# Segment sums in whole rounds of four blocks, message bases read behind the products, and one more picked tile in every third group of edges

## The reference, cut to what matters

```python
def _nnconv(x, src, dst, edge_attr, ew, eb, rw, rb):
    W = (edge_attr @ ew + eb).reshape(edge_attr.shape[0], x.shape[1], rw.shape[1])
    xj = x[src]
    msg = jnp.einsum('ei,eio->eo', xj, W)
    agg = jax.ops.segment_sum(msg, dst, num_segments=x.shape[0])
    return agg + x @ rw + rb
...
for i in range(N_LAYERS - 1):
    h = _nnconv(h, src, dst, edge_attr, edge_w[i], edge_b[i], root_w[i], root_b[i])
    h = _batchnorm(h, bn_gamma[i], bn_beta[i])
    h = jax.nn.relu(h)
h = _nnconv(h, src, dst, edge_attr, edge_w[-1], edge_b[-1], root_w[-1], root_b[-1])
```

## Time and profile before

| what | value |
|---|---|
| median of 3 runs | 7327.02 us (7326.24 to 7327.81) |
| profiled execution: its own time | 7327.42 us |
| its span, first to last instruction | 7325.4 us |
| mean granted TensorE clock, of 1 | 0.979 |
| PE busy | 7064.4 us (96%) |
| DVE busy | 6245.8 us (85%) |
| POOL busy | 5323.9 us (73%) |
| ACT busy | 4977.1 us (68%) |

### The profile page before, as it was taken

One profiled execution on the slowest core, in us unless ns is written; L12 is line 12 of the kernel. 1 busy time (PEld: TensorE's weight loads), 2 busy tenths in 40 slices (PEclk: granted clock), 3 DMA queues, 4 the chain that ended last, 5 costly groups with the idle time before them and its releaser, 6 DMA issues.

```text
span 7325.4 us, 131059 instructions
## 1 busy us (share of the span) xinstructions
PE 7064.4 (96%) x49442; PEld 6060.6 (83%) x49442; DVE 6245.8 (85%) x7568; ACT 4977.1 (68%) x8367; POOL 5323.9 (73%) x5635
## 2 busy tenths in 40 slices
PE   4999999999999899999999999989999999999998
PEld 3888888888888688888888888868888888888887
DVE  5888888888888788888888888878888888888885
ACT  4776667677767577676767677657767766676775
POOL 4777777777777477777777777757777777777774
PEclk7999999999999799999999999989999999999998
DMA  6111111111111111111111111111111111111111
GB/s 46 32 31 30 32 32 32 32 32 30 31 32 32 28 32 32 32 32 29 32 32 32 32 32 31 30 30 31 32 32 31 30 32 32 32 32 32 32 29 23
DMA packets 714221, 229.54 MB, mean 31 GB/s; under 512 B 573057, under 2 KB 664593, under 8 KB 713593
## 3 DMA queue, kind: packets, MB, share of 16 engines
q1 hardware_dynamic: 493253, 172.63, 10.6%
q0 software_dynamic: 180000, 46.44, 6.4%
q10 hardware_dynamic: 40340, 2.08, 0.7%
HBM read 217.19 MB, written 3.52 MB: 30 GB/s over the span
## 4 chain that ended last, share of the span: by engine, by line
PE 65%; POOL 17%; issue 8%; DVE 7%; DVEq 2%; ACT 0%; DMA 0%; POOLq 0%; ACTq 0%
PE bank L1128 52%; POOL xg L500 17%; PE bank L1095 8%; DVE xbig L688 2%; DVEq L778 2%; DVE spread L741 1%; DVE agg L783 1%; PE bank L1142 1%; PE bank L1141 1%; DVE agg L642 1%; PE bank L1199 1%; PE bank L1152 1%; PE bank L1154 1%; PE bank L1211 1%; DVE xg L746 0%
## 5 line engine op out<-in xcount | busy, mean ns | idle before, releaser
L500 POOL DMA_INDIRECT xg<-node_table,idx x5625 | 5323.1, 946 | 1927.5 <-issue 1777.3
L1128 PE MATMUL bank<-nodes,low_hot 128*128 128x448 f32 x26250 | 5632.5, 370 | 96.5 <-DVE spread L741 67.3
L1128 PEld LDWEIGHTS bank<-nodes,low_hot 128*128 128x128 f32 x26250 | 4860.5, 188 | 700.6 <-issue 191.7
L970 ACT ACTIVATE distance<-key_all,low_id 128x640 bf16<-128x640 int16 x3000 | 2242.0, 818 | 1840.0 <-issue 1213.2
L741 DVE TENSOR_TENSOR spread<-mask,bank 128x448 f32<-128x448 uint8 x3750 | 2168.5, 615 | 778.1 <-PE bank L1128 740.3
L976 ACT ACTIVATE low_hot<-distance,one 128x640 fp32r<-128x640 bf16 x3000 | 2233.0, 817 | 0.0
L746 DVE TENSOR_REDUCE xg<-spread 128x80 f32<-128x2240 f32 x750 | 1864.5, 2486 | 25.7
L688 DVE TENSOR_TENSOR xbig<-xg,bank 128x1280 f32<-128x1280 f32 x750 | 1329.6, 1810 | 20.9 <-DMA xg<-node_table,idx 19.7
L1095 PE MATMUL bank<-xbig,hot 128*32 128x144 f32 x18750 | 994.8, 295 | 0.0
L1095 PEld LDWEIGHTS bank<-xbig,hot 128*32 128x32 f32 x18750 | 820.7, 109 | 178.8 <-issue 115.7
L680 DVE TENSOR_TENSOR hot<-bank,dst_rel 128x800 f32<-128x800 f32 x375 | 367.8, 981 | 0.0
(11 more groups left out here) (115 smaller groups left out, 948.7 us busy)
## 6 DMA issues: line engine op xcount, KB each, us to landing
key_all<-edge_keys SPq DMA_DIRECT2D x375, 320.0 KB, 3.6
xg<-node_table,idx POOLq DMA_INDIRECT x5625
ea<-in_edge_attr SPq DMA_DIRECT2D x375, 100.0 KB
idx<-in_src SPq DMA_DIRECT2D x375, 7.5 KB
node_table<-rows_room SPq DMA_DIRECT2D x3, 781.2 KB
xbig<-node_table SPq DMA_DIRECT2D x3, 672.0 KB
xbig<-in_x SPq DMA_DIRECT2D x2, 781.2 KB
xbig<-in_src ACTq DMA_DIRECT2D x1, 937.5 KB
```

The lines of the kernel that those rows point to most:

```text
L500: pool.indirect_dma_start(out=xg[u][:, j, :], out_offset=None, in_=table[:, :], in_offset=bass.IndirectOffsetOnAxis(ap=idx[u][:, j:j + 1], ...
L970: nc.scalar.activation(distance[f][:, 0:tiles.stop - tiles.start, :], key[u % KEYS][:, tiles, :], ACT.Abs, bias=low_id[:, f:f + 1]).then_i ...
L1128: last = nc.tensor.matmul(p_sel[place_in_all % BANKS], low_hot[:, i // 2, t, :], nodes[:, i, :, :].rearrange("p d f -> p (d f)"), start=i ...
```

## The change

Three edits, with what they need in buffers:

1. **Sums by rounds.** `sum_tiles(g)`, which summed the five blocks of a group, becomes `sum_round(layer, r)`, which sums the four blocks of a round from the one or two groups they lie in. PE calls it at the end of its turn for each round that ends with group g. A block that doesn't fill a round waits for the next turn, so the target one-hots `hot` go from two buffers to three. The semaphore `s_seg` (groups summed) becomes `s_round` (rounds summed), and every wait on it is counted anew. In `before`, with five blocks on four strips of 32 columns, two blocks of each group share a strip.
2. **Bases.** The five reads into registers leave `add_quad` and stand at the head of the same turn of DVE: three behind `multiply_picked`, two behind `multiply_fetched`.
3. **Picks.** `PICKS` goes from 10 for every group to 10, 10, 11: the third, sixth, ... group picks eleven tiles and gathers fourteen (41 groups of 125). Places are counted from the end, so a group of ten starts at t = 1 of 0 to 10 and one of eleven at t = 0; the first half has 5 or 6 tiles, the second always 5. The places at which PE transposes (behind t = 1 and 3) and makes messages (behind t = 7) keep their numbers.

To make room, some small buffers share space with others. The diff, cut to its core:

```diff
-PICKS = (10,)
+PICKS = (10, 10, 11)
...
+    def first_pick(g):
+        return MOST - picks(g)
     def parts(g):
-        return slice(0, 5), slice(5, picks(g))
+        return slice(first_pick(g), HALF), slice(HALF, MOST)
...
-        hot = [sb(f"hot{i}", [P, TILES, WIN]) for i in range(PAIR)]
+        hot = [sb("hot0", [P, TILES, WIN])]
+        hot += [rows_room[:, i * TILES * WIN:(i + 1) * TILES * WIN].rearrange("p (t w) -> p t w", w=WIN)
+                for i in range(TRIPLE - 1)]
...
+        def stepped(k):
+            return k // G * R + rounds_done(k % G)
+        def summed(k):
+            return k // G * R + -(-(k % G + 1) * BLOCKS // GANG)
...
-                        pool.wait_ge(s_seg, layer * G + b * SLOTS + (u + 1))
+                        k = layer * G + b * SLOTS + u
+                        if k >= SLOTS:
+                            pool.wait_ge(s_round, stepped(k - SLOTS))
...
-                dve.wait_ge(s_seg, k + CREDIT - 1)
+                if k >= TRIPLE:
+                    dve.wait_ge(s_round, summed(k - TRIPLE))
                 n = (b * SLOTS + u) * BLOCKS
-                onehots(hot[k % PAIR][:], dst_rel[:, n:n + BLOCKS, :].rearrange("p n j -> p (n j)")).then_inc(s_hot, 1)
+                onehots(hot[(b * SLOTS + u) % TRIPLE][:], dst_rel[:, n:n + BLOCKS, :].rearrange("p n j -> p (n j)")).then_inc(s_hot, 1)
...
-            def add_quad(layer, q):
+            def read_bases(rounds):
+                return [dve.value_load(base_i[0:1, r:r + 1], min_val=0, max_val=N - 1) for r in rounds]
+            def add_quad(layer, q, bases):
                 rounds = quad_rounds(q)
-                bases = [dve.value_load(base_i[0:1, r:r + 1], min_val=0, max_val=N - 1) for r in rounds]
                 dve.wait_ge(s_mm, layer * QUADS + q + 1)
...
+                        ended = quad_rounds((g - 1) // QUAD) if g and ends_quad(g - 1) else range(0)
+                        under_picked = (len(ended) + 1) // 2
                         multiply_picked(layer, b, u)
+                        bases = read_bases(ended[:under_picked])
                         multiply_fetched(layer, b, u)
+                        bases += read_bases(ended[under_picked:])
...
                 for r in rounds_of(g):
                     n = layer * R + r
-                    act.wait_ge(s_seg, layer * G + g + (1 + CREDIT))
+                    act.wait_ge(s_round, n + 1)
...
-            def sum_tiles(g, buf, onehots):
+            def sum_round(layer, r):
+                n = layer * R + r
+                if n >= PAIR:
+                    pe.wait_ge(s_z, n - PAIR + 1)
+                blocks = range(r * GANG, min((r + 1) * GANG, NB))
                 for j in range(RUN):
-                    for a in range(BLOCKS):
-                        n, t = g * BLOCKS + a, a * RUN + j
-                        c = n % GANG
-                        done = nc.tensor.matmul(p_z[n // GANG % PAIR][c * WIN:(c + 1) * WIN, :], onehots[:, t, :],
-                                                buf[:, t, :], start=j == 0, stop=j == RUN - 1)
-                return done
+                    for at in blocks:
+                        g, t, c = at // BLOCKS, at % BLOCKS * RUN + j, at % GANG
+                        done = nc.tensor.matmul(p_z[r % PAIR][c * WIN:(c + 1) * WIN, :], hot[g % TRIPLE][:, t, :],
+                                                xw[(layer * G + g) % TRIPLE][:, t, :], start=j == 0, stop=j == RUN - 1)
+                done.then_inc(s_round, 1)
...
                         for t in range(MOST):
-                            if not (last and u == SLOTS - 1) and t < picks(g + 1):
+                            if not (last and u == SLOTS - 1) and t >= first_pick(g + 1):
                                 pick(layer, b, u + 1, t)
                             if t in (1, 3) and t // 2 < len(ended):
                                 transpose_round(layer, ended[t // 2])
...
-                        behind = layer * R + ((g + 1) * BLOCKS - 1) // GANG - 1
-                        if behind > 0:
-                            pe.wait_ge(s_z, behind)
-                        sum_tiles(g, xw[k % TRIPLE], hot[k % PAIR]).then_inc(s_seg, 1)
+                        for r in rounds_of(g):
+                            sum_round(layer, r)
```

More of the change, by code:

```diff
@@ L189, in gnn_kernel @@
         pb = sb("pb", [NODE_P, D])
-        col_i = sb("col_i", [P, P], I32)
+        col_i = spread[:].rearrange("p a b c -> p (a b c)")[:, 0:P].bitcast(I32)
         row_i = sb("row_i", [P, 1], I32)
@@ L207, in gnn_kernel @@
         ln_r = sb("ln_r", [NODE_P, PER])
-        bn_s = sb("bn_s", [D, CHUNKS, 6])
+        bn_s = spread[0:D, :, :, :].rearrange("p a b c -> p (a b c)")[:, 0:CHUNKS * 6].rearrange("d (c s) -> d c s", s=6)
         bn_m = sb("bn_m", [D, 2])
@@ L222, in gnn_kernel @@
         far_z = z[0][0:FAR_WIN, :]
[L223 to L224 removed]
+        far_zT = zT[:].rearrange("p q w -> p (q w)")[:, 0:FAR_WIN]
+        far_zxT = zxT[:].rearrange("p q w -> p (q w)")[:, 0:FAR_WIN]
         far_col = sb("far_col", [P, 1])
@@ L426, in load_keys @@
                 g = b * SLOTS + u
-                sp.dma_start(key[u % KEYS][:, 0:picks(g), :].rearrange("p t e -> p (t e)"),
-                             keys[g:g + 1, 0:picks(g) * P].to_broadcast([P, picks(g) * P])).then_inc(s_key[u], 16)
+                sp.dma_start(key[u % KEYS][:, first_pick(g):MOST, :].rearrange("p t e -> p (t e)"),
+                             keys[g:g + 1, first_pick(g) * P:MOST * P].to_broadcast([P, picks(g) * P])).then_inc(s_key[u], 16)
             AHEAD = 2
@@ L721, in set_masks @@
                 g = b * SLOTS + u
+                here = slice(first_pick(g), MOST)
                 n = picks(g)
@@ L725, in set_masks @@
                 nc.vector.tensor_tensor(
-                    mask[k % PAIR][:, 0:n, :], p_col[:, 0:FINE].unsqueeze(1).to_broadcast([P, n, FINE]),
-                    fine[:, g, 0:n].unsqueeze(2).to_broadcast([P, n, FINE]),
+                    mask[k % PAIR][:, here, :], p_col[:, 0:FINE].unsqueeze(1).to_broadcast([P, n, FINE]),
+                    fine[:, g, here].unsqueeze(2).to_broadcast([P, n, FINE]),
                     ALU.is_equal).then_inc(s_mask, 1)
@@ L735, in take_picks @@
                 t0, t1 = part.start, part.stop
-                before, fetched = picks_before(k), fetches(k % G)
+                before = picks_before(k)
                 dve.wait_ge(s_mask, k + 1)
@@ L739, in take_picks @@
                 for t in range(t0, t1):
-                    dve.wait_ge(s_pick, before + t + 1)
+                    n = before + t - first_pick(k % G)
+                    dve.wait_ge(s_pick, n + 1)
                     nc.vector.tensor_tensor(
@@ L753, in multiply_picked @@
                 dve.wait_ge(s_xg, k * 2 + 2)
-                dve.wait_ge(s_seg, k + CREDIT - 2)
+                if k >= TRIPLE:
+                    dve.wait_ge(s_round, summed(k - TRIPLE))
                 taken = slice(fetches(k % G), TILES)
@@ L814, in segments @@
                         if g and ends_quad(g - 1):
-                            add_quad(layer, (g - 1) // QUAD)
-                add_quad(layer, QUADS - 1)
+                            add_quad(layer, (g - 1) // QUAD, bases)
+                add_quad(layer, QUADS - 1, read_bases(quad_rounds(QUADS - 1)))
                 dve.wait_ge(s_add, layer * R + (R + CREDIT))
@@ L950, in copy_segments_far @@
                         act.wait_ge(s_fT, m + 1)
-                        nc.scalar.activation(far_zT[:], p_farT, ACT.Copy)
-                        nc.scalar.activation(far_zxT[:], p_farxT, ACT.Copy).then_inc(s_fzT, 1)
+                        nc.scalar.activation(far_zT, p_farT, ACT.Copy)
+                        nc.scalar.activation(far_zxT, p_farxT, ACT.Copy).then_inc(s_fzT, 1)
             def compare_keys(layer, b, u, half, between=None):
@@ L963, in compare_keys @@
                 if k:
-                    act.wait_ge(s_pick, picks_before(k - 1) + parts((k - 1) % G)[half].stop)
+                    act.wait_ge(s_pick, picks_before(k - 1) + parts((k - 1) % G)[half].stop - first_pick((k - 1) % G))
                 before = k * (4 * FOLD) + half * 2 * FOLD
@@ L984, in copy_picked_rows @@
                 act.wait_ge(s_xg, k * 2 + 2)
-                act.wait_ge(s_seg, k + CREDIT - 2)
+                if k >= TRIPLE:
+                    act.wait_ge(s_round, summed(k - TRIPLE))
                 taken = slice(fetches(k % G), TILES)
@@ L1162, in segment_sums @@
                 apart(pe)
-                for t in range(picks(0)):
+                for t in range(first_pick(0), MOST):
                     pick(layer, 0, 0, t)
```

25 lines of the change are left out of this document (12 added, 13 removed).

## The result

| | before | after |
|---|---|---|
| median | 7327.42 us (7326.24 to 7328.48, 4 runs) | 7418.74 us (7401.54 to 7430.24, 4 runs) |
| profiled execution, own time | 7327.42 us | 7401.54 us |
| its mean granted clock | 0.979 | 0.976 |

The ratio is 1.0122, with an interval of 1.011 to 1.0134: slower, by 91 us. The forecast was 7450, in a range of 7335 to 7490. The runs of after spread by 29 us, those of before by 2, and the profiled execution of after is the fastest of its four.

What follows compares the result with a forecast made beforehand. PE's loop was taken to set the time, with the gathers close behind. 7327.4 + 47 for the steps and gathers + 78 for falls of the clock = 7452, said as 7450 us, range 7335 to 7490.

Steps and rivals of the forecast that it cites:

- The sums: PE's sum of a plain step: a round takes 1.35 us in place of 2.57, with strips side by side.
- Rival D: PE's strips don't run side by side, a round takes 2.06 us: 7534 us; chance 0.10 with its milder form.
- its milder form: PE's rounds at 1.68 us by the skill's 3.07 times: 7444 us without falls; within the 0.10 of Rival D.
- The copy of z: Plain steps of ten: PE's transposition waits 0.7 us for ACT's copy in some 126 places, 88 us; step 17.19.
- rival C: About no change: z lands in time, additions don't, clock holds; plain steps 16.91, 0.28 less each, 7339 us; chance 0.08.
- The additions: Adding steps: DVE's additions start at 3.52 us, PE's transposition at 5.46 after a 2.8 us wait; ten picks stay 19.15.
- The picks: Steps of eleven: one more pick of 1.43 us; plain 18.4, double 21.12, adding 20.06; 123 fewer gathers give -10 us.
- Without the clock: All steps summed with no falls of PE's clock: +57 for three layers, -10 for gathers, +47 in all, 7374 us.
- The clock: PE's 2.8 us wait in 60 adding steps of ten lowers its clock: 1.3 us a step, +78 us.
- Rival A: PE's clock holds through the 2.8 us waits for additions: 7327 + 47 = 7374 us; chance 0.22.
- Rival B: Picks behind a waiting transposition start anyway, DVE's first spread sets PE's steps: faster, 7308 us; chance 0.08.

Runs made afterwards that it cites:

- the earlier z: Changed kernel with ACT's copy of a single round's sum behind two of the four absolute values instead of all four: 7435.33 us, ratio 1.0143.
- the bases alone: Kernel before with only the second edit, the reads of the bases moved behind the products: 7313.06 us, ratio 0.9978.
- the picks alone: Kernel before with the third edit (10, 10, 11 picks) and some small buffers sharing space: 7490.28 us, ratio 1.0221.
- the filled wait: Changed kernel with 14 matmuls of unread result ahead of the transposition in adding steps of ten: 7378.01 us, ratio 1.0067.
- fewer elevens: Changed kernel with transpositions and messages one pick later, and eleven picks in every fifth group instead of every third: 7260.81 us, ratio 0.991.
- elevens in plain steps alone: Changed kernel with transpositions and messages one pick later, and eleven picks only in groups 3, 7, 11 of sixteen: 7242.91 us, ratio 0.9882.

## Why the prediction was right, point by point

**The sums.** A round was put at 1.35 us and takes 1.36. A rule that spoke against it was the 3.07 times of the Trainium skill (TensorE: Matmul & The Clock Gate, Part 3: Packing small matmuls), by which 1.68 was estimated. This case's trace does not agree: 40 passes on four strips take 1.36 us where 50 with one strip used twice took 2.57, so the time goes by the fullest strip, ten passes against twenty, and the four strips run side by side. Rival D and its milder form fall with it.

**The copy of z.** The transposition was put at 3.38 us of the plain step and starts at 3.37, behind a wait of 0.69 in 126 places; the total was put at 88 us and is 87.5. Taking the copy forward gives 14 us, less than the 0.28 a step of rival C (35 us). Without the wait for z the plain steps of ten are 17.01 to 17.03 on the mean, not 16.91: in the earlier z all 126 of them wait for DVE's spread, as C has it, but the step that this leaves was put a tenth low.

**The additions.** Their transposition was put at 5.46 and starts at 5.45. That the reads cost nothing behind the products and let the additions start 0.5 earlier is shown from both sides: 0.58 a step gained in the bases alone, where the double steps of layer 1 stay at 19.69, and 0.54 and 0.59 lost with the reads put back.

**The picks.** Steps of eleven were put at 18.4, 21.12 and 20.06, and measured 18.52, 21.13 and 20.04. One quotient behind them is off: 8.76 / 6 is 1.46, not 1.43. It hardly matters, for in the picks alone an eleventh pick costs 1.40 to 1.46 by kind of step, but 0.03 on 123 picks are 4 us. The gathers, the other side of this edit, hold a small part of the chain before, and 53% of it once PE's steps are shorter and ten picks are kept.

**Without the clock** the sum was 7374. The filled wait, which has no falls and the same steps otherwise, took 7378. As the terms agree step by step, this isn't luck.

**The clock.** That the wait for the additions brings falls is shown: filling it and changing nothing else takes them all away. The size was off. The term of the prediction is "60 x 1.3 = +78"; measured are 29 us in the profiled execution (17 falls) and 41 at the median. This is nearly the whole miss of the forecast: 37 too much here, 4 too little in the rest. A fall was put at 1.65 us at most and took 1.7 on the mean, so 1.65 is no bound: three of the 17 lasted 6.8 us and made their steps some 2.9 longer. What was too large is their number, 78 / 1.65 = 47 of 60 where 17 came in the profiled execution and, by 41 / 1.7, an estimated 24 at the median. The prediction took most of the bound because its nearest row was a wait of 2.20 that did fall, and one case is not a share. Rival A, that the clock holds, was wrong in kind, and at 7374 it is 45 us from 7418.7, the forecast 31: the times alone would hardly have told them apart, the granted clock and the filled wait do.

**Rival B**, that picks behind a waiting transposition start anyway, is excluded: the nine picks of the plain step start at 719.60, behind the transposition that z held.

**What stays open.** Why the same wait brings a fall in one step and none in the next. In after it is 2.38 to 2.39 us in all 17 steps with a fall and in nearly all of the 43 without, so its length doesn't decide there. The number of falls also differs between executions of one kernel: the four of after took 7401.5, 7413.7, 7423.8 and 7430.2 us at granted clocks of 0.976, 0.975, 0.973 and 0.972, and 0.004 of 7420 us is 30, an estimate of what the clock took that covers the spread of 29. Why the earlier z has more falls than after is open as well. It may be a matter of how the waits lie in time; no run here set that on purpose.

## What to carry to other kernels

When an operation in an engine's ordered list gets shorter, look first at what each instruction behind it waits for: here 1.2 us saved in a sum came back as waits at a transposition, and moving that by one pick turned 7419 us into 7345. When PE waits for about two microseconds or more in each of many steps (here 1.8 to 2.9), look at the granted clock, price it beside the wait, and test it by filling the wait with matmuls whose result is not read. Work that is moved between engines to balance them is best put in the steps with room for it, and no more of it than the other engine's margin asks: fewer elevens took 7345 to 7261, and elevens in plain steps alone took it to 7243.

## What the runs showed of the hardware that was not expected

- Falls of the clock don't belong to one wait. They came at waits for additions (17 to 49 of 60 by kernel, at idle times of 2.4 to 2.9 us), for a spread (15 of 30, where PE was idle for 1.85 us in the step shown), and in plain steps where gathered rows were late (21). Some lasted 3.4 us and some 6.8.
- More work made PE's layer shorter: with 280 more matmuls in layer 1 (20 steps of 14), PE was busy for 34 us more by the windows above, and the layer took 13 us less from first to last sum.
- Moving a 0.27 us copy forward on ACT, a gain of 14 us by itself, came out 17 us slower instead (medians 7435.3 against 7418.7, with ranges that meet), with more falls in steps that it doesn't touch.
